# In the attention scores of a graph network, the turned one-hot matrices are made by VectorE from rows loaded onto all partitions, and TensorE's products run three groups ahead

## The reference

```
x_l = x @ Wl + bl ; x_r = x @ Wr + br          # (6250, 4 heads, 32)
m = leaky_relu(x_l[src] + x_r[dst] + weight * We, 0.2)
alpha = einsum('ehc,hc->eh', m, att)           # a score for each edge and head
alpha = softmax of alpha over the edges of each destination
out = segment_sum(x_l[src] * alpha, dst) + bias
```

## Time and profile before

| | us |
|---|---|
| median of 3 runs (lowest, highest) | 5697.41 (5667.19, 5700.05) |
| the profiled execution: time | 5702.34 |
| its span, first to last instruction | 5700.5 |
| scores stage in it | about 2361 to 3636 |
| busy: PE, DVE, ACT, POOL | 3324.1, 2808.7, 1675.3, 2048.7 |

### The profile page before, as it was taken

One profiled execution on the slowest core, in us unless ns is written; L12 is line 12 of the kernel. 1 busy time (PEld: TensorE's weight loads), 2 busy tenths in 40 slices (PEclk: granted clock), 3 DMA queues, 4 the chain that ended last, 5 costly groups with the idle time before them and its releaser, 6 DMA issues.

```text
span 5700.5 us, 61044 instructions
## 1 busy us (share of the span) xinstructions
PE 3324.1 (58%) x19159; PEld 3100.7 (54%) x19160; DVE 2808.7 (49%) x3801; ACT 1675.3 (29%) x2774; POOL 2048.7 (36%) x1982
## 2 busy tenths in 40 slices
PE   1300000019999999544444444357479999689697
PEld 0300000019999999544333343246379789589597
DVE  8300000024454544677666677788954344544345
ACT  0000000005645455200000000023266356456265
POOL 2777666750000000377677777346300000200300
PEclk9999999999999999755555555579789999799798
DMA  9700000008858587499899899247368268478585
GB/s 356 275 1 16 1 1 1 1 12 278 257 183 276 175 275 227 126 228 220 215 216 214 215 221 222 62 122 214 92 205 277 84 208 277 151 244 285 180 283 183
DMA packets 887483, 1008.44 MB, mean 177 GB/s; under 512 B 391651, under 2 KB 651705, under 8 KB 887270
## 3 DMA queue, kind: packets, MB, share of 16 engines
q1 hardware_dynamic: 795778, 861.50, 51.6%
q0 software_dynamic: 56208, 63.97, 4.8%
q10 hardware_dynamic: 35284, 80.30, 3.6%
HBM read 692.09 MB, written 233.14 MB: 162 GB/s over the span
## 4 chain that ended last, share of the span: by engine, by line
PE 44%; another core or an unknown queue 23%; DVE 14%; issue 11%; POOL 3%; ACT 2%; DMA 2%; DVEq 1%; SPq 0%; ACTq 0%; POOLq 0%
PE banks L918 35%; PE banks L841 4%; POOL work L624 2%; PE banks L1000 2%; DVE Z L1397 1%; DVE big L1519 1%; DVE Z L1402 1%; PE banks L863 1%; ACT banks L779 1%; DVE big L1406 1%; DMA work<-tab,stage 1%; DVE Z L1404 1%; ACT X L668 1%; PE banks L966 1%
## 5 line engine op out<-in xcount | busy, mean ns | idle before, releaser
L918 PE MATMUL banks<-wides,rows 128*128 128x384 f32 (+2 forms) x11040 | 2028.5, 344 | 155.8 <-issue 88.6
L918 PEld LDWEIGHTS banks<-wides,rows 128*128 128x128 f32 x11040 | 1949.4, 189 | 229.1 <-issue 94.3
L624 POOL DMA_INDIRECT work<-tab,stage x832 | 902.8, 1085 | 1483.0 <-ACT stage L771 1232.2
L1265 DVE CAST wides<-big 128x768 fp32r<-128x768 f16 (+3 forms) x1429 | 811.1, 569 | 1176.7 <-PE banks L918 1072.3
L698 ACT CAST wides<-big 128x768 fp32r<-128x768 f16 (+2 forms) x1037 | 832.2, 804 | 677.9 <-PE banks L918 554.3
L598 POOL DMA_INDIRECT cells<-queue_i x784 | 787.0, 1004 | 311.9 <-issue 298.6
L972 PE MATMUL banks<-V,work 128*128 x1664 | 372.5, 414 | 378.6 <-ACT work L773 312.1
L972 PEld LDWEIGHTS banks<-V,work 128*128 128x128 f32 x1664 | 345.1, 316 | 415.9 <-issue 415.9
L650 POOL DMA_INDIRECT V<-tab,nodei x100 | 96.2, 962 | 1201.9 <-DMA tab<-X 879.8
L863 PE MATMUL banks<-work 128*128 128x50 f16 x784 | 92.1, 278 | 670.6 <-issue 600.5
L863 PEld LDWEIGHTS banks<-work 128*128 128x128 f16 x784 | 73.1, 149 | 689.5 <-issue 612.6
(11 more groups left out here) (300 smaller groups left out, 3229.1 us busy)
## 6 DMA issues: line engine op xcount, KB each, us to landing
big<-cells SPq DMA_DIRECT2D x490, 416.0 KB
big<-cells SPq DMA_DIRECT2D x441, 384.0 KB
big<-turned SPq DMA_DIRECT2D x300, 384.0 KB
gathered<-work SPq DMA_DIRECT2D x104, 512.0 KB
work<-gathered SPq DMA_DIRECT2D x104, 512.0 KB, 4.2
big<-turned SPq DMA_DIRECT2D x100, 416.0 KB
cells<-work ACTq DMA_DIRECT2D x98, 416.0 KB, 14.6
turned<-big SPq DMA_DIRECT2D x50, 800.0 KB
```

Of the source, the lines that this page charges most:

```text
L624: pool.indirect_dma_start(msg[:, j, u, :], None, tab[0][:, :], bass.IndirectOffsetOnAxis(ap=stage[:, j * U + u:j * U + u + 1].bitcast(U32) ...
L918: last = pe.matmul(banks[:, 4 * (w % 2) + j, 0:(z - a) * P], rows2[:, s, part * D:(part + 1) * D], wides[:, q % QUEUE, (a - start) * P:(z ...
L1265: dve.tensor_copy(wides[:, (2 * m + 1) % QUEUE, 0:(z - a) * P], halves[:, m % HALVES, a * P:z * P]).then_inc(s_wided, 1)
```

## The change

relR is stored once in DRAM as fp16 (rel_rows, one row of 128 to a visit; values over 1024 are cut to 1024, which matches no place). In the scores SP loads the 8 rows of a group, 2 KB, onto all 128 partitions; VectorE compares them with its partition number (pcol) and has the turned one-hot matrices at once, as picks[j], four buffers in the place of the former diag and oh. TensorE's transposes, ScalarE's copy and their semaphores go. The products' PSUM tile takes all 8 banks, a ring of 4 groups, and TensorE may be 3 groups ahead (LEAD). VectorE's turn g begins with the one-hot matrices of group g+3; SP's turn g begins with a wait for these, and loads the row of group g+5 into one of two buffers.

```diff
@@ -86,6 +86,7 @@
+        rel_rows = dram("rel_rows", (VP, P), H16)
@@ -143,7 +144,7 @@
-        ps = banks[:, 0:4, :].rearrange("p (h b) (u f) -> p h (b u) f", h=2, f=P)
+        ps = banks[:, :, :].rearrange("p (h b) (u f) -> p h (b u) f", h=RING, f=P)
@@ -202,8 +203,8 @@
-        s_oT = sem("s_oT")
-        s_oTc = sem("s_oTc")
+        s_rel = sem("s_rel")
+        s_row = [sem(f"s_row{j}") for j in range(2)]
@@ -244,6 +245,7 @@
+        rel16 = Vf[:, 5 * VP + COLS:5 * VP + COLS + VP // 2].bitcast(H16)
@@ -268,6 +270,10 @@
+        LEAD = RING - 1
+        rows_at = RING * MOSTT // 2
+        row_in = big[:, rows_at:rows_at + U * P].bitcast(H16).rearrange("p (k e) -> p k e", k=2)
+        assert rows_at + U * P <= EXT0 and (GROUPS + LEAD + 2) * U <= VP and 5 * VP + COLS + VP // 2 <= CT * P
@@ -279,6 +285,7 @@
+        picks = [diag[:, 0], diag[:, 1], oh[:, 0], oh[:, 1]]
@@ -503,6 +510,18 @@
+            def load_row(first, k):
+                sp.dma_start(row_in[:, k, :], rel_rows[first, :].rearrange("(a u) e -> a (u e)", a=1).to_broadcast([P, U * P])).then_inc(s_row[k], 16)
+
+            for n in range(LEAD + 2):
+                if n >= 2:
+                    sp.wait_ge(s_oh, n - 1)
+                load_row(slice(n * U, (n + 1) * U), n % 2)
+
+            def next_row(i, j):
+                sp.wait_ge(s_oh, i * RING + (j + LEAD + 1))
+                load_row(bass.ds(i * (RING * U) + (j + LEAD + 2) * U, U), (j + LEAD + 2) % 2)
+
@@ -511,6 +530,7 @@
+                    next_row(i, j)
@@ -745,6 +766,8 @@
+            act.wait_ge(s_go, go("rows A"))
+            act.dma_start(rel_rows.rearrange("(g p) e -> p g e", p=P), rel16.rearrange("p (g e) -> p g e", g=VT)).then_inc(s_rel, 16)
@@ -769,8 +792,6 @@
-                    act.wait_ge(s_oT, i * RING + (j + 1))
-                    act.copy(diag[:, j % 2, :, :], pm[:, j % 2, :].rearrange("p (u f) -> p u f", f=P)).then_inc(s_oTc, 1)
@@ -962,14 +983,10 @@
-                    for u in range(U):
-                        last = pe.transpose(pm[:, j % 2, u * P:(u + 1) * P], oh[:, j % 2, u, :], ident[:, :])
-                    last.then_inc(s_oT, 1)
...
-                    pe.wait_ge(s_oTc, i * RING + (j + 1))
-                    pe.wait_ge(s_add, i * (RING * U) + (j * U + ADD0 - U))
+                    pe.wait_ge(s_add, i * (RING * U) + (j * U + ADD0 - LEAD * U))
...
-                        last = pe.matmul(ps[:, j % 2, u, :], diag[:, j % 2, u, :], Vf[:, bass.ds(t * P, P)], start=True, stop=True)
+                        last = pe.matmul(ps[:, j, u, :], picks[j][:, u, :], Vf[:, bass.ds(t * P, P)], start=True, stop=True)
@@ -993,7 +1010,7 @@
-                    pe.wait_ge(s_oh, i * RING + (GROUPS + 1 + j + 1))
+                    pe.wait_ge(s_oh, i * RING + (GROUPS + LEAD + j + 1))
@@ -1198,6 +1215,7 @@
+            link(dve.tensor_scalar(rel16, relR.rearrange("p g e -> p (g e)"), 1024.0, None, ALU.min))
@@ -1221,6 +1239,7 @@
+            dve.wait_ge(s_rel, 16)
@@ -1377,23 +1396,22 @@
-            def onehot(rel, first, j, at):
-
-                dve.wait_ge(s_mm, at)
-                dve.tensor_tensor(oh[:, j % 2, :, :], over(iota_f[:, 0:P], U),
-                                  rel[:, first].rearrange("p (u o) -> p u o", o=1).to_broadcast([P, U, P]),
-                                  ALU.is_equal).then_inc(s_oh, 1)
+            def onehot(j, at):
+                dve.wait_ge(s_row[j % 2], at)
+                dve.tensor_scalar(picks[j % RING].rearrange("p u f -> p (u f)"), row_in[:, j % 2, :], pcol[:, 0:1], None, ALU.is_equal).then_inc(s_oh, 1)
...
-            onehot(relA, slice(0, U), 0, RING)
+            for n in range(LEAD):
+                onehot(n, 16 * (n // 2 + 1))
...
-                    onehot(relA, bass.ds(g8 + (j + 1) * U, U), j + 1, i * RING + (j + RING))
+                    dve.wait_ge(s_mm, i * RING + (j + RING))
+                    onehot(j + LEAD, i * (16 * RING // 2) + 16 * ((j + LEAD) // 2 + 1))
...
-                    dve.tensor_tensor(sc_a, ps[:, j % 2, :, :], msg[:, j, :, :], ALU.add).then_inc(s_p1, 1)
+                    dve.tensor_tensor(sc_a, ps[:, j, :, :], msg[:, j, :, :], ALU.add).then_inc(s_p1, 1)
@@ -1408,6 +1426,8 @@
+            for k in range(2):
+                dve.wait_ge(s_row[k], 16 * ((GROUPS + LEAD + 3 - k) // 2))
@@ -1498,7 +1518,7 @@
-            dve.wait_ge(s_oh, GROUPS + 1)
+            dve.wait_ge(s_oh, GROUPS + LEAD)
```

## The result

The changed kernel took 5643.33 us (median of 9 runs, 5632.66 to 5658.90), the kernel before 5700.05 in its 9 runs on the same chip: ratio 0.990, 95% interval 0.988 to 0.992. It is 1% faster where 1% slower was forecast. The time lies inside the stated range of 5590 to 5890 us only because that range kept half of rival A; the forecast itself went the wrong way. The profiled execution took 5635.9 us, with a span of 5634.0 against 5700.5: 66.5 us less.

A forecast was written before the change was run, and what follows sets the result against it. A closed ring between SP and VectorE was to bound the scores at 12.7 us a group: +50 for 99 turns, +11.6 start, -4 end, +0.6 preparation, +58 on 5702.3, 5760, or 5755 against the median; range 5590 to 5890 us.

The forecast's parts named there:

- rival A: Scores: short ring of 10.9 us, DMA share partly waiting, GpSimd's 10.7 to 11.1 us bounds; 5577 us, chance 0.17.
- the ring's sum: Scores, per group: SP and VectorE legs add to 12.4 us, plus 0.3 for the row load, 12.7 us.
- the transpose's issue: SP's leg in the scores: 6.4 us from when SP is free, 4.9 where the queue was almost empty.
- closed ring: Scores: SP waits for VectorE's one-hot, VectorE for SP's store, with no overlap between turns; 12.7 us a group.
- one-hot to transpose: Scores, first legs: one-hot 0.7 us, SP's wake-up 0.1, row load's issue 0.7.
- store to next one-hot: Scores: from the store's issue to VectorE's next one-hot, 4.3 us, from above 7.8.
- queueing behind the row: SP's queue in the scores: row load ahead of transpose and store adds 0.3 us, a third of its 0.9.
- the stage's term: Scores, 99 turns at 12.7 us instead of 12.19: +50 us.
- The floor of the DMA engines: Scores: 11.3 us of work a group plus 0.9 for the row load, 12.2, at 0.99 share 12.3 us.
- "remote" releaser: Scores: late TensorE hand-overs (ScalarE 542.5 us, VectorE 167.0) go; products up to three groups (36 us) early hide late releases.
- Start: Opening of the scores: first rows, one-hots, transpose and store delay VectorE's second turn, +11.6 us.
- end: Close of the scores: the last four groups have no transpose and save about 4 us.

The follow-up runs named there:

- pause_no_row: Changed kernel without row loads in the loop, ScalarE staging every second group after GpSimd issued the group ahead, in four copies: 5135.70 us, 0.9941 (kernel before 5164.71).
- pause_in_before: Kernel before, ScalarE staging every second group only after GpSimd issued the group ahead, in four copies: 5163.51 us, 0.9996 (kernel before 5164.71).
- store_wait_scalare: Changed kernel with the wait for the store moved from VectorE to ScalarE, before it stages: 5307.68 us, 1.0276 (kernel before 5166.99).
- after_fourth: Changed kernel, unaltered, run as a control on a chip where the kernel before takes 5163.69 us: 5222.93 us, ratio 1.0112.
- sp_row_again: Changed kernel with SP's one-hot wait and row load moved behind the store: 5179.18 us, 1.0024 (kernel before 5164.71).
- no_row_loads: Changed kernel that counts rows as loaded in the loop without loading them, all waits kept: 5744.26 us, 1.0000 (kernel before 5746.33).
- after_again: Changed kernel, unaltered, run again on a chip where the kernel before takes 5746.33 us: 5679.08 us, ratio 0.9884.
- landed_in_before: Kernel before, GpSimd waiting in every second group until its gathers of the group ahead have landed: 5785.42 us, 1.0062 (kernel before 5751.27).
- save_a_turn_later: Changed kernel with SP's row load behind the store and each save behind the next group's store: 5729.94 us, 0.9973 (kernel before 5746.33).
- rows_as_bytes: Changed kernel with rows kept and loaded as bytes, 128 KB a load instead of 256 KB: 5215.19 us, 1.0094 (kernel before 5163.69).

## Why the prediction was wrong

**The step that failed** is one term of the ring's sum, the transpose's issue. That there would be a closed ring, and its order, were right: VectorE waits 3.2 us for the store in 95 turns ("about 3 us" forecast), the transpose follows the one-hot by 1.53 us in the median turn (1.5), the second turn opens at 2399.57 (2399.7). Leg by leg, forecast and measured mean:

| | forecast | measured |
|---|---|---|
| one-hot to transpose | 1.5 | 1.90 |
| transpose's issue | 6.4 | 4.93 |
| to the store | 0.2 | 0.34 |
| store to next one-hot | 4.3 | 4.34 |
| queueing behind the row | 0.3 | inside the issue |
| sum | 12.7 | 11.51 |

The transpose's issue is the term that was mis-sized, by 1.5 us of 6.4. I had both ends and took the wrong one. The 6.4 us of the earlier trace rows is an issue into a queue in which a store and a save had just been put; it is high even there, for the 100 issues of that trace have a mean of 5.04 us. The 4.87 of the earlier trace rows is one into a nearly empty queue, and a closed ring leaves the queue so. I used just that argument for the landing time, and not for the leg beside it. That the issue grows with what is queued shows in the mean issues: 3.54 us where SP had put nothing into its queue for 3.8 us (pause_no_row), 6.24 where a save had been put in 0.3 us before and a store 1.2 (pause_in_before), 6.8 where it was a row load 0.2 us before and a save 0.9 (store_wait_scalare). With a group at 11.51 us in place of 12.7, the stage's term is 99 x (11.51 - 12.24) = -72 instead of +50.

Two errors hide in that one number and partly cancel. In a closed ring without row loads the issue is 3.54 us, 2.9 under the forecast's 6.4; behind a row load it is 5.34 (after_fourth), 1.8 more, where I had allowed 0.3 for queueing. That the sum came as near as 1.2 us is in part luck. Both figures are from 5165 chips; on the chip of the result only the 4.93 was measured.

**The floor of the DMA engines was none.** I read 0.92 x 12.2 as 11.2 us of work per group, added 0.9 for the row, and held 12.2 as a floor against the faster cases. The changed kernel moves more bytes in 11.51 us at a share of 1.01. sp_row_again, on a 5165 chip, moves the same bytes in 11.05 at 1.15 (from 2080 to 3160 us). The share counts the time packets are under way and passes 1. It also pushed down rival A, whose condition (ring of 10.9, share partly waiting) was half met: its 4.9 us transpose came true.

**Where the gain comes from** I had half right. The closed ring takes 11.5 to 11.7 us a group on every chip. That is a loss against the 10.9 of the kernel before on a 5165 chip, and a gain against its 12.2 to 12.3 on a 5700 one, where it waits for a "remote" releaser some 50 times. The sum expected these waits to go because TensorE works three groups ahead. The lead is worth 0.3% (0.9916 against 0.9885, with intervals that overlap), and in no_row_loads it doesn't hold stretches of 40 us. But TensorE's signals still come late in the changed kernel: of those recorded, 16 by over 2 us in the result's profile (96 us in all, at most 13.1), 28 in after_again (264 us, at most 21.4). They stay under the 36 us of the lead, and VectorE's add waits for a "remote" releaser 0 and 2.3 us in these two; in no_row_loads the latest is 38.8 us, and the add waits 270.4 us. So the ring keeps the lateness short and the lead hides what is left. That the ring does this through GpSimd's pace, with 44 pauses of 0.9 us or more in after_again against 14 in no_row_loads, is an inference from no_row_loads, landed_in_before and the times of the late signals.

One rival was not tested by itself: the kernel before hands work from TensorE to the others twice a group (turned matrices, products), the changed one once. That can't be all of it, for no_row_loads and save_a_turn_later have the one hand-over and a faster ring, and on a 5700 chip they gain 0.0 and 0.3%. No run has the two hand-overs with the new ring.

**Smaller steps.** Start +14.0 (forecast 11.6), end -3.0 (-4). GpSimd's gathers went from 1085 to 1061 ns, as forecast from the shorter one-hot. The one-hot takes 0.75 us (0.70). SP's wait for transposes to land (63.6 us in 30 saves) I had left out, but it doesn't make 1.90 of 1.5: in after_fourth it is 218.2 us in 99 saves, and the leg has a mean of 1.49. The excess shows on the 5700 chips only (2.22 in after_again), where SP's steps are late at times.

The estimate of 3.8 us for the store's landing from the Trainium skill, DMA: Bandwidth & Descriptors, section "Anatomy of one DMA — SWDGE (gpsimd) path", fell short of the 4.34 us measured; that section is on DMAs that GpSimd issues, and SP issued this one.

In the result's profile the gathers that start inside the new one-hot take 1.13 us (mean of 37), against 0.96 for those that start while VectorE is idle and 1.48 for those that started inside L1383 before. So the new form still delays GpSimd, but less than the old one. The Trainium skill, SBUF — State Buffer, section "Who interferes with whom", says that tensor_scalar can block GpSimd for the whole instruction; the longest of these 37 took 1.57 us, a delay of 0.6 us, which fits that and doesn't prove it.

**Still open:** why TensorE and SP slow down on the 5700 chips and not on the 5165 ones, whether the late signals of the kernel before and the slow stretches of no_row_loads are one thing, and whether it is GpSimd's rate or the length without a pause that starts it. In after_again one stretch (2834 to 2852) began in spite of pauses of 1.0 and 1.6 us in the 30 us ahead of it.

## What to carry to other kernels

When a wait closes a ring, take every leg of it from turns in which the queue is as empty as the ring will leave it, and from the mean of many, not from one row. An engine's late releases can go with a neighbour's unbroken pace, so ask of a gain whether it comes from the edit or from the throttle that the edit puts in; then a control on a chip without the disturbance can turn its sign, as here from -1.0% to +1.1%. A busy share of the DMA engines is not work per item: don't build a floor on it.

## What the hardware showed that I hadn't expected

Chips differ by 10% on the same program. On a 5700 chip VectorE's loop in the first 900 us waits in steps of some 21 us, while GpSimd issues one indirect DMA after another (there it scatters into the matrix of edge counts). Between 200 and 888 us of the changed kernel's span:

```profile
DVE work L1210 <- remote: 600.9, 31, 22.1
```

after_fourth, on a 5165 chip, has 478 of these scatters in the same window, the changed kernel here 485, and after_fourth has no "remote" wait. In the slow stretch shown TensorE starts one matmul in 2.1 to 3.9 us and SP's steps are late, while GpSimd's gathers go on with gaps of 0.3 us.

Late signals of TensorE come when GpSimd pauses: 43 of 46 in landed_in_before.

A load that repeats eight rows onto 128 partitions costs the transpose queued behind it 1.8 us, at 256 KB and at 128 KB alike (5.34 and 5.30 us in after_fourth and rows_as_bytes against 3.54 in pause_no_row, all on 5165 chips).
